# Transposed weights from the host and a reordered first batch in an LN + FFN + attention kernel

## The reference

```python
xn = layernorm(x)
# FFN half
routing   = softmax(xn @ gate_w.T)                 # 8 experts
in_scale  = routing @ in_channel_scale             # (tokens, 1024)
out_scale = routing @ out_channel_scale
ffn = (xn * in_scale) @ sign(weight).T * out_scale + bias
g = silu(ffn)
# attention half: 16 heads of 64, rotary, causal softmax, output projection
s = attention(xn, Wq, Wk, Wv, Wo)
out = x + s * g
```

## Time and profile before

| what | value |
|---|---|
| median of 3 runs | 1188.04 us (1187.37 to 1189.5) |
| the profiled execution, its own time | 1189.66 us |
| span of the profiled execution | 1187.4 us |
| mean granted TensorE clock | 0.984 |
| PE busy | 1142.3 us (96%) |
| DVE, ACT, POOL busy | 729.4, 616.2, 432.1 us |

### The profile page before, as it was taken

How to read it: one execution, slowest core, us unless ns; L and a number is a source line. 1 busy time by engine, 2 the same in 40 slices (tenths; PEclk the granted TensorE clock), 3 DMA queues, 4 the chain that set the end, 5 groups by cost and what they waited for, 6 DMA issues and landing times.

```text
span 1187.4 us, 17857 instructions
## 1 busy us (share of the span) xinstructions
PE 1142.3 (96%) x5736; PEld 954.0 (80%) x5736; DVE 729.4 (61%) x1735; ACT 616.2 (52%) x1291; POOL 432.1 (36%) x258
## 2 busy tenths in 40 slices
PE   4699999999999999999999999999999998999998
PEld 3477777788888888888888888888888886888886
DVE  7676553357776777767767777767767777323133
ACT  5445344155666556656566466655665666322111
POOL 2526427433433424235333343342523523332220
PEclk9799999999999999999999999999999998999999
DMA  6734232302202022021460220202202025555652
GB/s 205 283 107 189 77 107 76 120 0 73 62 9 62 9 71 62 9 62 36 176 212 9 69 59 13 62 9 71 62 9 62 26 72 186 164 182 179 209 196 104
DMA packets 86983, 111.23 MB, mean 94 GB/s; under 512 B 3304, under 2 KB 68840, under 8 KB 85936
## 3 DMA queue, kind: packets, MB, share of 16 engines
q1 hardware_dynamic: 86960, 110.93, 28.7%
HBM read 77.37 MB, written 33.55 MB: 93 GB/s over the span
## 4 chain that ended last, share of the span: by engine, by line
PE 87%; DVE 6%; ACT 3%; POOL 2%; issue 1%; DMA 1%; SPq 0%; DVEq 0%; ACTq 0%; POOLq 0%
PE at_proj L44 17%; PE at_proj L46 17%; PE at_proj L45 17%; PE at_out L909 7%; PE at_pt L896 6%; PE ff_z_ps L264 6%; PE at_score L878 3%; PE at_score L879 3%; PE at_score L44 2%; PE at_score L45 2%; PE at_score L46 2%; PE at_proj L863 1%; POOL ff_xs_lo L601 1%; DMA w_stage<-in_L_ffn_weight_dram 1%; ACT xn_hi L365 1%
## 5 line engine op out<-in xcount | busy, mean ns | idle before, releaser
L44 PE MATMUL at_proj<-xn_hi,w_hi 128*128 128x512 f32 x896 | 363.4, 406 | 2.9 <-ACT at_v_t L1014 2.9
L46 PE MATMUL at_proj<-xn_hi,w_lo 128*128 128x512 f32 x896 | 352.0, 393 | 0.0
L45 PE MATMUL at_proj<-xn_lo,w_hi 128*128 128x512 f32 x896 | 350.8, 392 | 0.0
L46 PEld LDWEIGHTS at_proj<-xn_hi,w_lo 128*128 128x128 f32 x896 | 169.0, 189 | 37.6
L44 PEld LDWEIGHTS at_proj<-xn_hi,w_hi 128*128 128x128 f32 x896 | 169.5, 189 | 33.3 <-issue 3.3
L45 PEld LDWEIGHTS at_proj<-xn_lo,w_hi 128*128 128x128 f32 x896 | 169.8, 190 | 30.4
L1273 POOL TENSOR_TENSOR at_turning<-at_turning,rope_table 128x512 f32<-128x512 f32 x64 | 82.9, 1296 | 305.1 <-DVE at_turning L1144 305.1
L1281 POOL TENSOR_TENSOR w_lo<-w_stage,w_hi 128x1024 fp32r<-128x1024 f32 x45 | 114.5, 2559 | 162.8 <-ACT w_hi L993 162.8
L1031 ACT ACTIVATE at_prob<-at_score,at_neg_max 128x512 f32<-128x512 f32 (+3 forms) x256 | 133.4, 526 | 68.0 <-DVE at_neg_max L1172 67.6
L1040 ACT ACTIVATE at_pt_hi<-at_pt 128x512 fp32r<-128x512 f32 (+1 forms) x192 | 94.0, 524 | 101.1 <-PE at_pt L896 100.4
L1189 DVE TENSOR_TENSOR at_pt_lo<-at_pt,at_pt_hi 128x512 fp32r<-128x512 f32 (+1 forms) x192 | 111.8, 597 | 43.7 <-ACT at_pt_hi L1040 42.8
(11 more groups left out here) (129 smaller groups left out, 1827.7 us busy)
## 6 DMA issues: line engine op xcount, KB each, us to landing
z_store<-z SPq DMA_DIRECT2D x16, 512.0 KB, 2.7
w_stage<-in_L_attn_Wq_dram SPq DMA_DIRECT2D x16, 512.0 KB, 3.8
w_stage<-in_L_attn_Wk_dram SPq DMA_DIRECT2D x16, 512.0 KB, 5.1
w_stage<-in_L_attn_Wv_dram SPq DMA_DIRECT2D x16, 512.0 KB, 6.1
att_store<-at_att_t SPq DMA_DIRECT2D x32, 256.0 KB, 2.0
rope_table<-att_store SPq DMA_DIRECT2D x16, 512.0 KB, 6.5
z<-_attn_hidden_states_dram SPq DMA_DIRECT2D x16, 512.0 KB, 4.5
at_turning<-z_store SPq DMA_DIRECT2D x16, 512.0 KB, 6.1
```

What stands on the lines that cost most here:

```text
L44: pe.matmul(out, sh, mh, start=first, stop=False)
L45: pe.matmul(out, sh, ml, start=False, stop=False)
L46: return pe.matmul(out, sl, mh, start=False, stop=final)
```

## The change

The host passes `weight` transposed and `gate_w` laid out as 128 x 64. The kernel no longer transposes either: ACT takes signs of the weight straight into the matrix that ffn reads, one row piece for each slice k, and ffn of tile 0 waits for the sign of slice k before it. The sign copies of ACT and DVE and the transposes of PE go. The gate weights are loaded into a buffer of their own and rounded by ACT as its first instruction.

The channel tables are rounded by POOL instead of ACT, and the low parts made on 64 partitions in one instruction. Rows 32 and 64 of the routing operand change roles to fit. The x tiles 2 and 3 are loaded ahead of the weight; the input table goes between them and the weight. Each of x tiles 1 to 3 has PSUM banks that are its own until ffn starts, or (tile 3) those of tile 1.

The order of batch 0 is a new one: PE runs ffn of tiles 0 and 1 without work for batch 1 in between, and all four x_transposes, gate, and the router's transposes of batch 1 stand within and around ffn of tiles 2 and 3. The layer norm of tiles 4 and 5 moves on DVE behind all eight `scale` of batch 0, and its root on ACT behind the last sign. Batches 1 to 3 keep their order. `ROUNDS` still gives rounds of four tiles.

```diff
+ROUNDS = tuple((j, 0, QT) for j in range(BATCH))
+        X_BANKS = {1: 1, 2: 0, 3: 1}
...
             load(0)
             load(1)
+            load(2)
+            sp.dma_start(gate_raw[:].rearrange("p k e -> p (k e)"), io["gate_t"]).then_inc(gate_in, 16)
+            load(3)
+            sp.wait_ge(chan_zero, 1)
+            load_table(0)
             load_rows(0)
-            load(2)
-            load(3)
             load_rows(1)
...
+            load_table(1)
+            load(4)
             load_rows(2)
-            load_rows(3)
-            load(4)
             load(5)
-            for t in range(4, KT):
+            for t in range(3, KT):
                 load_rows(t)
...
+                    if k == 0 and n < 2:
+                        pe.wait_ge(x_lo, (6, 8)[n])
+                    elif k == 0:
                         pe.wait_ge(z_mul, n - 1)
...
+                    if n == 0:
+                        pe.wait_ge(signed, k + 1)
...
-            sign_transposes(0)
             x_transposes(0)
-            sign_transposes(1)
             x_transposes(1)
-            gate_w_transposes()
             x_transposes(2)
             x_transposes(3)
...
+            for k in range(KT):
+                ffn(0, (k,))
+                if k + 4 < KT:
+                    in_scale(0, k + 4)
+            ffn(1, range(KT))
...
+                if j == 0:
                     x_transposes(m)
+                    ffn(2, range(1))
                     x_transposes(m + 1)
+                    ffn(2, range(1, 4))
                     x_transposes(m + 2)
+                    ffn(2, range(4, 6))
                     x_transposes(m + 3)
+                    ffn(2, range(6, KT))
+                    gate(1)
+                    ffn(3, range(2))
+                    gate_transposes(1)
+                    ffn(3, range(2, 4))
...
-                act.activation(w_sign[:, t % 2, :], w_rows[:, t % 2, :], ACT.Sign).then_inc(signed, 1)
+                act.activation(keep["sign_t"][:, t, :], w_rows[:, t % 2, :], ACT.Sign).then_inc(signed, 1)
...
+            gate_w_high()
+            ln_root(0, 2)
             sign(0)
+            ln_root(1, 2)
             x_high(0)
             x_high(1)
             x_high(2)
             x_high(3)
+            gate_copy(0)
+            sign(1)
+            parts_copy(0)
+            route_exp(0)
+            sign(2)
+            route_copy(0)
+            xs_high(0, range(2))
             sign(3)
+            xs_high(0, range(2, 4))
+            out_scale(0, 0)
             sign(4)
+            xs_high(0, range(4, 6))
             sign(5)
+            xs_high(0, range(6, KT))
             sign(6)
             sign(7)
+            out_scale(0, 1)
+            ln_root(2, 2)
+            out_scale(1, 0)
+            out_scale(1, 1)
...
+                if j == 0:
+                    x_high(m)
+                    out_scale(2, 0)
+                    x_high(m + 1)
+                    ln_root(3, 2)
+                    out_scale(2, 1)
+                    x_high(m + 2)
+                    x_high(m + 3)
...
             layer_norm(0)
+            gate_w_low()
             layer_norm(2)
             x_low(0)
             x_low(1)
             x_low(2)
             x_low(3)
+            router(0)
+            scale(0, range(KT))
             layer_norm(4)
+            z_scale(0)
...
+                if j == 0:
+                    x_low(m)
+                    z_scale(1)
+                    layer_norm(m + 2)
+                    x_low(m + 1)
+                    x_low(m + 2)
+                    x_low(m + 3)
+                    z_scale(2)
+                    layer_norm(m + 4)
+                    router(1)
+                    scale(1, range(4))
+                    z_scale(3)
+                    continue
...
+            def channel_table(c):
+                table = keep[("chan_in", "chan_out")[c]]
+                pool.wait_ge(chan_in_sem[c], 4 * 16)
+                pool.tensor_copy(table[:], chan_rows[:, c, :]).then_inc(chan_hi, 1)
                 pool.wait_ge(chan_hi, c + 1)
+                pool.tensor_tensor(table[64:P, :], chan_rows[64:P, c, :], raw(table[64:P, :]), ALU.subtract).then_inc(chan_lo, 1)
+                pool.wait_ge(chan_lo, c + 1)
```

More of the change, by code:

```diff
@@ L113, in ffn_block, with tokens, tiles_in @@
         z_out = keep["z_out"]
+        ALL_SCALED = KT * len(ROUNDS)
+        def tokens(r):
+            return slice(ROUNDS[r][1] * P, ROUNDS[r][2] * P)
+        def tiles_in(r):
+            return QT * ROUNDS[r][0] + ROUNDS[r][2]
         @block.sync
@@ L129, in load_rows, with load_table @@
                     sp.wait_ge(signed, t - 1)
[L130 removed]
+                sp.dma_start(w_rows[:, t % 2, :], io["weight_t"][t * P:(t + 1) * P, :]).then_inc(w_in[t % 2], 16)
+            def load_table(c):
+                for r in range(4):
+                    sp.dma_start(chan_rows[32 * r:32 * r + EXPERTS, c, :], (io["in_scale"], io["out_scale"])[c])\
+                      .then_inc(chan_in_sem[c], 16)
             def store_xn(j):
@@ L367, in x_high, with gate_copy, parts_copy, route_exp @@
                         act.wait_ge(scaled, KT * j)
-                    act.activation(xn_full[:, ks, tok], x_bank(n, b), ACT.Copy).then_inc(x_hi, 1)
-            def gate_copy(j):
-                act.wait_ge(gate_mm, j + 1)
-                act.activation(logit_t[:], small_ps[0:2 * EXPERTS, :], ACT.Copy).then_inc(gate_sb, 1)
-            def parts_copy(j):
-                act.wait_ge(gate_tr, j + 1)
-                act.activation(parts[:].rearrange("p t e -> p (t e)"), small_ps[:, 0:QT * 2 * EXPERTS], ACT.Copy).then_inc(gate_sb, 1)
-                act.wait_ge(shifted, j + 1)
-                act.activation(route_e[:], route[:], ACT.Exp).then_inc(expd, 1)
-            def route_copy(j):
-                act.wait_ge(route_tr, j + 1)
-                act.activation(route_t[:, j % 2, :], small_ps[:], ACT.Copy).then_inc(route_sb, 1)
-            def xs_high(j, ks):
+                    act.activation(xn_full[:, ks, tok], x_bank(n, b), ACT.Copy).then_inc(x_full, 1)
+            def gate_copy(r):
+                width = tokens(r).stop - tokens(r).start
+                act.wait_ge(gate_mm, r + 1)
+                act.activation(logit_t[:, 0:width], small_ps[0:2 * EXPERTS, 0:width], ACT.Copy).then_inc(gate_sb, 1)
+            def parts_copy(r):
+                count = ROUNDS[r][2] - ROUNDS[r][1]
+                act.wait_ge(gate_tr, r + 1)
+                act.activation(parts[:, 0:count, :].rearrange("p t e -> p (t e)"), small_ps[:, 0:count * 2 * EXPERTS],
+                               ACT.Copy).then_inc(gate_sb, 1)
+            def route_exp(r):
+                count = ROUNDS[r][2] - ROUNDS[r][1]
+                act.wait_ge(shifted, r + 1)
+                act.activation(route_e[:, 0:count, :], route[:, 0:count, :], ACT.Exp).then_inc(expd, 1)
+            def route_copy(r):
+                toks = tokens(r)
+                act.wait_ge(route_tr, r + 1)
+                act.activation(route_t[:, ROUNDS[r][0] % 2, toks], small_ps[:, 0:toks.stop - toks.start], ACT.Copy)\
+                   .then_inc(route_sb, 1)
+            def xs_high(r, ks):
+                j, toks = ROUNDS[r][0], tokens(r)
                 for k in ks:
-                    act.wait_ge(scaled, KT * j + k + 1)
+                    act.wait_ge(scaled, KT * r + k + 1)
                     if j >= 1:
@@ L429, in _ @@
                 m = n + QT
+                if j == 0:
[6 more added lines that the diff above has]
+                    x_high(m + 3)
+                    ln_root(4, 2)
+                    gate_copy(1)
+                    out_scale(3, 0)
+                    parts_copy(1)
+                    route_exp(1)
+                    out_scale(3, 1)
+                    route_copy(1)
+                    xs_high(1, range(4))
+                    continue
                 out_scale(n, 0)
@@ L530, in router @@
                 else:
                     dve.wait_ge(route_zero, 1)
-                dve.tensor_copy(route4[:, :, 0:EXPERTS], route[:])
-                then(dve.tensor_copy(route4[:, :, 32:32 + EXPERTS], route[:]))
-                for c in (64, 96):
-                    dve.tensor_tensor(route4[:, :, c:c + EXPERTS], route[:], raw(route4[:, :, 0:EXPERTS]),
+                dve.tensor_copy(route4[:, 0:count, 0:EXPERTS], rt)
+                then(dve.tensor_copy(route4[:, 0:count, 64:64 + EXPERTS], rt))
```

351 lines of the change are left out of this document (158 added, 193 removed).

## The result

The changed kernel takes 1193.55 us (median of 8 runs, 1192.28 to 1199.47); the kernel before, on the same chip, 1188.37 (8 runs, 1186.74 to 1190.52). The ratio is 1.0048, with a 95% interval of 1.0031 to 1.0066: slower by 5.2 us (the difference of the medians) to 5.7 (by the ratio; 3.7 to 7.8 with the interval), which is more than can be put down to measurement, and less than the 8.1 forecast. The profiled execution of the changed kernel is its longest, 1199.47 with a span of 1197.5. A second profile of the same program is of an execution of 1192.17 (span 1190.1), and what follows goes by both.

A forecast was written before the change was run, and what follows sets the result against it. PE matmul time, 87% of the chain, was taken to bound the kernel. 11.4 us lost from tile 1 to tile 4 less 3.3 gained at the start gave 8.1 on 1188.04, rounded to 1196; range 1190.5 to 1200.5.

The forecast's parts named there:

- the likeliest case: Whole kernel: the forecast itself, a median of 1192 to 1198.5 us, chance 0.62.
- (a): First layer-norm root on ACT, behind gate-weight load, rounding and table load: at about 9.8, 2.8 us later than before.
- (b): Root to gate: POOL's table work holds DVE for 4.3 us; gate at 29.0 (24.7 to 33), against 26.05.
- (c): Gate to route transposes: slower gate and a sign, but the router starts at once; route transposes at 40.0, before 40.54.
- (d): Route transposes to first FFN matmul: 3.2 us to xs_high, 2 more to FFN, at 45.2, 4.4 us earlier.
- (e): FFN of tile 0 can't end before the last sign: tile 1 at 57.3, against 60.64, 3.3 us gained.
- Tile 1 to tile 4: Stretch between these tiles' output-scale matmuls: PE waits, half clock and added transposes lose 11.4 us on the 33.9 before.
- the wait at tile 6: PE's transposes of tile 6 wait for x_low of tile 5, behind the layer norm of tiles 6 and 7: 4.4 us.
- my own sign: Forecast is wrong if tile 4 starts before 96, or its shift there isn't the shift at the end.
- the start gives nothing: Rival: POOL holds DVE for 7, gate at half clock, tile 1 at 60.5, whole 11.4 lost: 1200 us, chance 0.22.
- it cancels: Rival: tile 1 at 52 to 54 and 8 us lost from there to tile 4: 1186 to 1190, chance 0.10.
- the start wins: Rival: gate at 22, tile 1 at 49.5, 11 us gained at the start: about 2 us faster, 1186, chance 0.06.

The follow-up runs named there:

- the three edits of the start: Changed kernel with first root ahead of gate weights, channel tables on POOL behind the fourth x low half, signs early, new order kept: 1187.58 us.
- changed again: The changed kernel run once more without edit, for a second profiled execution (1192.17 us): median 1194.72 us, ratio 1.0067.

## Why the prediction came out as it did

The mechanism was right, with both signs: a start that gains (2.3 us alone, 3.3 forecast), an order that loses more (8.4 to 9.7, 11.4 forecast). 1193.55 lies 2.5 below the 1196.0, inside the likeliest case. That it lies so near is partly luck: as the terms below show, waits put too high and costs put too low cancel in part.

(a) First root: 9.8 forecast, 10.08 and 9.12 in two executions. The root starts 1.29 behind the start of its table load, as in the row that the forecast went by. Moving the root ahead of the gate weights gave 2.0 us.

(b) Gate: 29.0 forecast, 30.56 and 27.34. I had taken POOL's roundings at the 2.4 of a subtraction; in the two profiles they take 1.04 and 1.54. The holds taken at 4.3 were 5.7 and 3.5, and putting them out of the way gave 3.5 us of time. The upper bound of 9 counted all of POOL's work as cost; that work took 7.1 in the first profile, and statistics beside it were not held in the second.

(c) Gate to route transposes: 11.0 forecast, 10.4 and 10.6. (d) To the first FFN matmul: 5.2 forecast, 5.1. Both held.

(e) FFN of tile 0: 12.1 forecast, 13.6 in the first profile and 12.2 in the second, the signs 6 and 7 ahead of their slices as said. Tile 1: 57.3 forecast, 59.71 and 55.28. That was the term with the widest real spread, and its two profiled values lie on both sides.

Tile 1 to tile 4: 11.4 forecast, 44.44 - 33.90 = 10.5 measured, 8.4 to 9.7 in the whole time. Of the terms, the wait at tile 6 was 4.05 (4.4 forecast), shown to be the layer norm by moving it; output scale 0 or 1.2 (1.6); tile 5 0.7 (1.2); tile 7 and gate 0.5 to 0.6 (1.1); route 1.1 (1.7); in-scale 0.2 (0.9). These come to 6.6 and 7.7, against 10.9. The clock was mis-sized the other way: 0.7 forecast. In the profile of 1192.17 in the windows 76 to 78 and 78 to 80 the clock is 0.62 and 0.52, which costs 2 x 0.38 + 2 x 0.48 = 1.7; in the first profile there are two such stretches, with windows at 0.50 from 60 to 62 and from 80 to 82, some 2.7 in all. How this term hangs on the wait at tile 6 the prediction had only as a guess (0 to 1.7): with the wait gone, the clock stayed at 1.00. Slower matmuls with xs as operand add 6 half tiles of 0.12, so 0.7, which I did not foresee at all. With the 0.8 of transposes added and the 1.0 of before taken off, this comes to 9.8 and 9.9; the last 0.6 to 0.7 of the 10.5 I can't place.

Behind tile 4 I had a constant shift. The changed kernel loses another 1.0 us up to the last half tile, and the passage into the attention block then takes 55.1 to 57.7 us, by whether the clock drops there. The profile of the kernel before, on which the sum was made, was one of the long passages. In the profile of 1192.17 this alone returns 2.6 us.

So the step that failed is the last one, the constant shift behind tile 4, by which the 8.1 at tile 4 was to be the 8.1 at the end. By my own sign I was wrong there. At tile 4 the two profiles are 9.6 and 5.2 later than before, at the end 10.1 and 2.7; in the medians it is 5.2 to 5.7.

The rival "the start gives nothing" comes near the longest execution (1199.47, tile 1 at 59.71), and fits no typical one; "it cancels" (tile 1 at 52 to 54, 1186 to 1190) wanted POOL's holds near nothing, and with the tables out of the way that is what came, 52.26 and 1190.08; "the start wins" (1186) would have needed the gate at 22, which the three edits of the start reached (22.62), with the result 1187.58.

## What to carry to other kernels

When two tiles' worth of matmul are run in a block at the front, what used to run beside them (layer norms, low halves) is left with too little beside it later: count, for each transpose, which vector work must lie between it and the one before. Large work on POOL is best started where DVE runs none of the operations that it holds (here elementwise ones on SBUF operands, not the statistics), even if its inputs are there sooner. Ask of a wait what the clock does behind it: taking 3.3 us of waits away gave 4.3. And a milestone in mid-program is not the end: read two executions before an early milestone is taken as a fixed shift.

## What the runs showed of the hardware

- A 0.16 us operation of DVE took up to 2.19 us while POOL ran a subtraction of 64x1024, and none of them did once POOL ran it at another time. Two BATCH_NORM_STATS2 of 128x512 beside such a subtraction took their usual 1.26.
- POOL's rounding copy of 128x1024 takes 1.04 us (1.54 and 1.63 in two profiles), its subtraction of 64x1024 2.34 to 2.68.
- After the same wait of 2.9 us at the passage into the attention block, PE is at 1.2 GHz for about 6 us in one execution (before, 235.4 to 241.4) and stays at 2.4 GHz in another (changed again). This moves the time by up to 2.8 us (55.01 to 57.84 over all profiles).
- Behind a wait of 4.04 us in mid-program the granted clock was 0.62 and 0.52 in the next two windows of 2 us; with that wait cut to 0.4, it stayed at 1.00.
- The same matmul form takes some 7 ns more in the changed kernel, with nothing in its form or waits to show for it; moving xs_hi by 32 bytes took back a quarter, in two versions.
